# The first way back of an alignment kernel: a part of each step moves from VectorE to TensorE and PSUM

## The reference, cut to what matters

```python
def _pairwise_euclidean(a, b): ...          # D[i, j], 64 x 1601 for each batch
def _dtw_cost(D): ...                       # R[i, j] = D[i, j] + min(R[i-1, j], R[i, j-1], R[i-1, j-1])
def _backtrack(R, T1, T2):                  # from (T1-1, T2-1) back to (0, 0)
    ...
    choice = jnp.argmin(jnp.stack([cd, cu, cl]))      # diagonal, up, left
    ni = jnp.where(choice <= 1, i - 1, i)
    nj = jnp.where((choice == 0) | (choice == 2), j - 1, j)
def _align_one(small, large):
    ...
    expanded = jnp.zeros((T_large, d)).at[j_idx].add(small[i_idx] * valid)
x = x + vmap(_align_one)(ctx_1024, layernorm(x))
x = x + rwkv7(layernorm(x), ...)
x = x + moe_ffn(layernorm(x), ...)
```

## Time and profile before

| what | value |
|---|---|
| median of 3 runs | 1171.64 us |
| span of the profiled execution | 1175.4 us (3.8 above the median, 0.9 above the slowest of the runs) |
| PE busy | 1005.5 us, 86% |
| DVE busy | 660.5 us, 56% |
| ACT busy | 494.2 us, 42% |
| chain that ended last, by engine | PE 55%, DVE 29%, DMA 6%, issue 4%, ACT 3% |
| share of that chain on L841 / L846 | 3% / 2.8% (both ways back) |
| way back of group 0 on DVE | 293.3 to 376.6 us |

### The profile page before, as it was taken

One profiled execution on the slowest core, in us unless ns is written; L12 is line 12 of the kernel. 1 busy time (PEld: TensorE's weight loads), 2 busy tenths in 40 slices (PEclk: granted clock), 3 DMA queues, 4 the chain that ended last, 5 costly groups with the idle time before them and its releaser, 6 DMA issues.

```text
span 1175.4 us, 15523 instructions
## 1 busy us (share of the span) xinstructions
PE 1005.5 (86%) x4892; PEld 598.2 (51%) x4892; DVE 660.5 (56%) x2311; ACT 494.2 (42%) x847; POOL 115.5 (10%) x150
## 2 busy tenths in 40 slices
PE   5886639888891799997899699887999999999998
PEld 2332213333330455553576465645676767676776
DVE  4994949999999776487669612427311111111116
ACT  4885627766781345423242155243222222222221
POOL 1000000000000000000000000000252425242210
PEclk9998979999996799988899799799999999999999
DMA  9999954565876989440050097394121212123115
GB/s 354 324 309 272 274 155 141 154 190 157 237 225 163 327 252 329 135 150 11 1 186 1 0 336 249 104 349 174 49 83 57 83 56 84 56 84 105 32 52 182
DMA packets 123806, 190.47 MB, mean 162 GB/s; under 512 B 9008, under 2 KB 93136, under 8 KB 123728
## 3 DMA queue, kind: packets, MB, share of 16 engines
q1 hardware_dynamic: 117840, 171.13, 47.0%
q0 software_dynamic: 5888, 18.36, 5.1%
HBM read 165.43 MB, written 24.03 MB: 161 GB/s over the span
## 4 chain that ended last, share of the span: by engine, by line
PE 55%; DVE 29%; DMA 6%; issue 4%; ACT 3%; SPq 2%; POOL 0%; DVEq 0%; ACTq 0%; POOLq 0%
PE bank L1816 13%; PE bank L1663 8%; PE bank L1847 7%; PE bank L1684 4%; DVE table L825 4%; PE bank L1808 3%; DMA spaced<-dist 3%; DVE beyond L841 3%; DVE passed L846 3%; PE bank L1827 3%; DVE col_min L818 2%; DVE z L756 2%; PE bank L1590 2%; PE bank L1839 2%; PE bank L1811 2%
## 5 line engine op out<-in xcount | busy, mean ns | idle before, releaser
L1028 DVE TENSOR_TENSOR hid<-bank,act_s 128x352 f32<-128x352 f32 x104 | 54.2, 524 | 220.9 <-PE bank L1816 182.1
L1816 PE MATMUL bank<-w_up,srcT 128*128 x512 | 162.9, 460 | 0.8 <-ACT srcT L1434 0.8
L1574 PE MATMUL bank<-sq,ones 128*64 128x402 f32 (+1 forms) x512 | 101.3, 517 | 38.2 <-ACT sq L1291 38.2
L1442 ACT ACTIVATE act_s<-bank 128x352 f32<-128x352 f32 x104 | 47.9, 463 | 198.4 <-PE bank L1816 127.7
L1816 PEld LDWEIGHTS bank<-w_up,srcT 128*128 128x128 f32 x512 | 96.0, 189 | 47.9 <-issue 4.1
L1590 PE MATMUL bank<-table,ident 128*128 128x402 f32 x144 | 68.5, 560 | 56.3 <-DVE stays L789 51.0
L1568 PE MATMUL bank<-ctxT,latT 128*64 128x402 f32 (+1 forms) x512 | 101.2, 517 | 4.8 <-DMA ctxT<-ctx_tr_dram 4.0
L1663 PE MATMUL bank<-rows_c,on_path 128*64 128x256 f32 (+1 forms) x832 | 100.8, 395 | 2.4 <-DMA rows_c<-ctx_nat_dram 1.6
L1291 ACT ACTIVATE sq<-ctxT 128x1608 f32<-128x1608 f32 x64 | 97.5, 1526 | 8.5 <-DMA ctxT<-ctx_tr_dram 8.5
L1847 PE MATMUL bank<-w_dn,hidT 128*128 (+1 forms) x384 | 93.6, 380 | 0.4 <-DVE y_sb L1042 0.4
L1328 ACT ACTIVATE code<-bank,unpassed 128x402 bf16<-128x402 f32 x72 | 42.1, 589 | 122.9 <-PE bank L1592 122.9
(11 more groups left out here) (292 smaller groups left out, 1619.5 us busy)
## 6 DMA issues: line engine op xcount, KB each, us to landing
rows_c<-ctx_nat_dram SPq DMA_DIRECT2D x32, 896.0 KB
ctxT<-ctx_tr_dram SPq DMA_DIRECT2D x32, 804.0 KB, 8.7
ctxT<-ctx_tr_dram SPq DMA_DIRECT2D x32, 797.0 KB, 7.5
rows_c<-ctx_nat_dram SPq DMA_DIRECT2D x32, 640.0 KB
spaced<-dist SPq DMA_DIRECT2D x128, 101.0 KB, 3.8
w_up<-w_t_dram SPq DMA_DIRECT2D x16, 704.0 KB, 13.3
table<-spaced SPq DMA_DIRECT2D x48, 202.0 KB, 4.2
w_dn<-w_t_dram SPq DMA_DIRECT2D x16, 256.0 KB, 5.8
```

The costliest lines, as they stand in the source:

```text
L1028: e.tensor_tensor(hid[i][:, :], psum[2 * i + 1][:, 0:HH], act_s[i][:, :], ALU.mult).then_inc(hid_done, 1)
L1574: last = e.matmul(ps[b * T:(b + 1) * T, 0:nq], ones[:, 0:T], sq[i][:, b, k, 0:nq], start=False, stop=(k == KC - 1))
L1816: last = e.matmul(psum[2 * i + m][:, 0:HH], srcT[t % 2][:, k, :], w_up[:, bass.ds(ex, 1), m, k, columns], start=(k == 0), stop=(k == KC - 1))
```

## The change

For group 0 only, L841 and its f32 sum go. TensorE now forms code plus twice the position in PSUM (`lay_pair`): an identity in bf16 (`alike`) times the code of two steps, then a product over two partitions (`spot_of`, `spot`) that adds the position, counted from the middle. One call lays the two steps of a pair in one of three banks (psum 5 to 7), and pair k waits until VectorE has finished pair k - 3. VectorE's comparison is one `tensor_scalar` in fp16 on positions counted from the middle (`row_mid`): -60000 where the position is at or above the threshold, 0 elsewhere; the reduction takes `hidden` from SBUF and the sum from PSUM. `threshold0` is fp16. Group 1's way back is as before. Three operations join VectorE's set-up and five join GpSimd's.

```diff
@@ VectorE, align(g) @@
-                e.memset(th[:, STEPS:SLOTS], 2.0 * N + 1).then_inc(back_done, 1)
+                e.memset(th[:, STEPS:SLOTS], 2.0 * N + 1 - (0 if g else MIDDLE)).then_inc(back_done, 1)
                 done()
+                if g == 0:
+                    for k in range(BACK_PAIRS):
+                        for at, step in enumerate(pair_steps(k)):
+                            old, new = th[:, step + 1:step + 2], th[:, step:step + 1]
+                            e.wait_ge(back_done, done.n)
+                            e.stream_shuffle(hidden[:, L:LW], old, RIGHT).then_inc(back_done, 1)
+                            e.tensor_scalar(hidden[:, 0:L], row_mid[:, :], old, -60000.0, ALU.is_ge,
+                                            ALU.mult).then_inc(back_done, 1)
+                            if at == 0:
+                                e.wait_ge(laid, k + 1)
+                            e.wait_ge(back_done, done(2))
+                            i = step % 2
+                            e.tensor_tensor_reduce(passed[:, :], hidden[:, :], back_bank(k)[:, i * LW:(i + 1) * LW], 1.0,
+                                                   -60000.0, ALU.add, ALU.max, new).then_inc(back_done, 1)
...
@@ VectorE, set-up @@
+            e.tensor_copy(alike[:, :], ident[:, :]).then_inc(set_up, 1)
+            e.tensor_scalar(inject0[:, :], inject[:, :], -float(MIDDLE), None, ALU.add).then_inc(set_up, 1)
+            e.tensor_scalar(row_mid[:, :], row2[:, 0:L], -float(MIDDLE), None, ALU.add).then_inc(set_up, 1)
@@ TensorE, align(g) @@
-                for step in range(STEPS):
-                    yield
+                for j in range(STEPS):
+                    if g == 0:
+                        ahead = range(BACK_BANKS) if j == 0 else [BACK_BANKS + j // 2] if j % 2 else []
+                        for k in ahead:
+                            if k < BACK_PAIRS:
+                                lay_pair(k)
+                    yield
+
+            def lay_pair(k):
+
+                steps = pair_steps(k)
+                r0, n, bank = steps[-1], len(steps), back_bank(k)[:, 0:len(steps) * LW]
+                if k == 0:
+                    e.wait_ge(spotted, 5)
+                    e.wait_ge(barred, HALVES)
+                e.wait_ge(coded, r0 // CB + 1)
+                if k >= BACK_BANKS:
+                    e.wait_ge(back_done, back_value(pair_steps(k - BACK_BANKS)[-1]))
+                e.matmul(bank, alike[:, :], code[0][:, r0:r0 + n, 0:LW], start=True, stop=False)
+                e.matmul(bank, spot_of[0:2, :], spot[0:2, 0:n, :], start=False, stop=True).then_inc(laid, 1)
```

More of the change, by code:

```diff
@@ L71 @@
 PASSED = 4096.0
+MIDDLE = SEGS * L
+BACK_BANKS = 3
 HALVES = 2 * CODES
@@ L209, in half_count, with pair_steps, back_value @@
     return g * HALVES + 2 * q + h + 1
+def pair_steps(k):
+    return [STEPS - 1] if k == 0 else [STEPS - 2 * k, STEPS - 1 - 2 * k]
+BACK_PAIRS = (STEPS + 1) // 2
+def back_value(step):
+    return 1 + 3 * (STEPS - step) + max(0, STEPS - max(T, step + 1))
 def dist_slot_value(u):
@@ L329, in build @@
         threshold_at = cursor[0]
-        threshold = [place(f"threshold{g}", [SLOTS]) for g in range(GROUPS)]
+        threshold = [place("threshold0", [SLOTS], F16), place("threshold1", [SLOTS])]
         after = cursor[0]
@@ L383, in build @@
             code.append(place(f"code{g}", [SLOTS, W], BF16))
+        at(table_at[0] + TABLE)
+        alike, spot, spot_of = place("alike", [P], BF16), place("spot", [2, LW], BF16), place("spot_of", [P], BF16)
+        inject0, hidden, row_mid = place("inject0", [STEPS]), place("hidden", [LW], F16), place("row_mid", [L], F16)
+        assert cursor[0] <= table_at[1]
         at(table_at[1])
@@ L503, in build @@
         numbered, shaped, terms_kept, terms_in = sem("numbered"), sem("shaped"), sem("terms_kept"), sem("terms_in")
+        spotted, laid = sem("spotted"), sem("laid")
         x_in = sem("x_in")
@@ L529, in build @@
         BUILT = 17
-        SET_UP = 11
+        SET_UP = 14
         TABLE_IN = [16 * -(-STEPS // FEW_ROWS) * sum(len(sets) for sets in LOADED_WITH[:g + 1]) for g in range(GROUPS)]
@@ L540, in path_bank, with back_bank @@
             return psum[2 + part]
+        def back_bank(k):
+            return psum[5 + k % BACK_BANKS]
         def code_rows(g, q, h):
@@ L579, in gpsimd_program @@
                 e.memset(stays[i][:, :, L:LW], 0.0).then_inc(built, 1)
+            e.memset(spot[0:2, :, :], 2.0 * L).then_inc(spotted, 1)
+            iota(spot_of[0:2, :], [[0, GB], [1, SEGS]], -(SEGS // 2), 0).then_inc(spotted, 1)
+            e.wait_ge(spotted, 2)
+            iota(spot[0:1, :, 0:L], [[0, 2], [2, L]], 2, 0).then_inc(spotted, 1)
+            e.memset(spot[0:2, :, L:LW], 0.0).then_inc(spotted, 1)
+            e.memset(spot_of[0:1, :], 1.0).then_inc(spotted, 1)
             def clear_table(g):
@@ L685, in vector_program @@
             e.tensor_scalar(tie[:, :], ident[:, :], -TIE, None, ALU.mult).then_inc(set_up, 1)
+            e.wait_ge(set_up, SET_UP - 3)
+            e.tensor_copy(alike[:, :], ident[:, :]).then_inc(set_up, 1)
+            e.tensor_scalar(inject0[:, :], inject[:, :], -float(MIDDLE), None, ALU.add).then_inc(set_up, 1)
+            e.tensor_scalar(row_mid[:, :], row2[:, 0:L], -float(MIDDLE), None, ALU.add).then_inc(set_up, 1)
             e.wait_ge(set_up, SET_UP)
@@ L834, in align @@
                 done(g * BACK_INCS)
-                e.memset(th[:, STEPS:SLOTS], 2.0 * N + 1).then_inc(back_done, 1)
+                e.memset(th[:, STEPS:SLOTS], 2.0 * N + 1 - (0 if g else MIDDLE)).then_inc(back_done, 1)
                 done()
+                if g == 0:
[12 more added lines that the diff above has]
+                                                   -60000.0, ALU.add, ALU.max, new).then_inc(back_done, 1)
+                            assert done() == back_value(step)
+                            if step >= T:
+                                e.wait_ge(back_done, done.n)
+                                e.tensor_tensor(new, new, inject0[:, step:step + 1], ALU.max).then_inc(back_done, 1)
+                                done()
+                            yield
+                    assert done.n == BACK_INCS
+                    e.wait_ge(back_done, done.n)
+                    path_features(0)
+                    return
                 for step in range(STEPS - 1, -1, -1):
@@ L903, in path_features @@
                                         passed[:, 0:T])
-                e.stream_shuffle(lim, threshold[g][:, 0:T + 1], FIRST_LANE).then_inc(termed, 1)
+                ends, middle = (lim, 0.0) if g else (hidden[:, 0:T + 1], float(MIDDLE))
+                e.stream_shuffle(ends, threshold[g][:, 0:T + 1], FIRST_LANE).then_inc(termed, 1)
                 e.wait_ge(termed, n())
-                e.tensor_scalar(lim, lim, 1.0, -1.0 - MID, ALU.max, ALU.add).then_inc(termed, 1)
+                e.tensor_scalar(lim, ends, 1.0 - middle, middle - 1.0 - MID, ALU.max, ALU.add).then_inc(termed, 1)
                 e.wait_ge(termed, n())
```

## The result

The changed kernel takes 1184.19 us (median of 8 runs, 1180.69 to 1187.86) beside 1175.2 us for the kernel before in the same comparison (8 runs, 1171.23 to 1181.32): a ratio of 1.0079, 95% interval 1.0060 to 1.0098, some 9 us slower. The profiled executions span 1186.6 and 1175.4 us. The forecast was slower by 4.0, 1175.6 us, with a range of 1169.0 to 1181.0; the sign was right, the size was less than half of what came, and the time lies above the range.

What follows compares the result with a forecast made beforehand. VectorE bounds the stretch at 4.75 us a unit, TensorE afterwards at 5.19. The last refinement comes 5.8 us later, the tail gains 1.8: +4.0 on 1171.64 gives 1175.6 us, range 1169.0 to 1181.0.

Steps and rivals of the forecast that it cites:

- First shuffle of the way back: Set-up: added operations delay the first layer norm by up to 1.0 us, hidden by full DMAs.
- The start: Start of group 0's way back: first reduction 2.05 us late behind pair 0, unit 52's products 3.7 us late.
- The unit: TensorE's unit in the stretch: two pairs of 0.40 us raise it from 4.39 to 5.19 us.
- The end of the stretch: Unit 63's products at 358.2, then pairs, leftovers and a wait for VectorE's step; last refinement at 367.1 us.
- The tail: VectorE's 15 last steps at 0.82 instead of 0.94 us gain 1.8 us; features take 3.43 as before.
- the change of bound from VectorE to TensorE: In the stretch of units, the bound passes from VectorE at 4.75 us a unit to TensorE at 5.19.
- the wait for context that goes: TensorE's wait for unit 56's context vanishes but gives nothing, as TensorE is late by more.
- the bank that costs the reduction nothing: VectorE's reduction reading PSUM instead of SBUF costs about nothing, bounds -0.05 to +0.10 us.
- rival C: VectorE's reduction from a bank is 0.12 us slower, so a step gains nothing: +5.8, 1177.4 us; chance 0.10.
- the table that is not waited for: Group 1's table moves by 5.8 to 382.8 us and stays 1.2 us ahead of VectorE.
- rival B: TensorE bounds but loses less: pair 0.27 us, or pairs keep the code halves' clock up; +1.1, 1172.7 us; chance 0.28.
- Rival A: Pairs cost TensorE almost nothing, running in gaps: -4.8 us, 1166.8 us; faster below 0.22 us a pair; chance 0.17.

Runs made afterwards that it cites:

- e6: Changed kernel with the position product over all 128 partitions, the other weights zero: ratio 1.0081, median 1184.67 us.
- e7: e6 with VectorE's three added set-up operations moved behind its first layer norm: ratio 1.0035, median 1180.16 us.
- e8: e7 with GpSimd's added set-up operations moved later as well: ratio 1.0041, median 1179.01 us.
- e10: e8 with the pairs from the fourth on laid two steps later in TensorE's order: ratio 1.0021, median 1177.24 us.
- e1_setup: Kernel before with only the added set-up operations on VectorE and GpSimd: ratio 1.0017, median 1178.15 us.
- e4: Changed kernel without each pair's position product, so positions are left out of the sum: ratio 1.0024, median 1177.31 us.
- e9: Changed kernel with the pairs from the fourth on laid two steps later in TensorE's order: ratio 1.0056, median 1181.32 us.
- e2: Kernel before with the set-up and TensorE's pairs, which nothing reads and which wait for nothing of VectorE's way back: ratio 1.0067, median 1183.01 us.
- e3: Changed kernel without TensorE's pairs, the reduction reading the code from SBUF, positions left out: ratio 0.9974, median 1173.86 us.
- e5: No pairs on TensorE; GpSimd adds the positions to the code in SBUF, VectorE does the last piece: ratio 1.0251, median 1205.14 us.

## Why the prediction was right in sign and short in size

At group 1's way forward the forecast was +4.0 and the trace has +11.5. The 7.5 us between them, term by term:

- *First shuffle of the way back, forecast no shift: +2.5 us.* I had let full DMAs hide the set-up, "at worst 1.0 shows". The layer norm was 1.33 late. Only some 0.5 of that were VectorE's three operations (e6 against e7); the rest was a thing I had called harmless, GpSimd's operations (e7 against e8). How much of it reached the way back I can't tell, since e8 and e10 start like the kernel before and are 1.8 and 3.0 us late at 160 us: the 2.5 us are in part, perhaps wholly, scatter between executions. What gives such a delay back, in e1_setup, is the wait for unit 56's context; the pairs remove that wait, so in the changed kernel it stays.
- *The start, forecast 5.15 us from first reduction to unit 52's products: 6.73, +1.7 with 0.1 at the first reduction.* That pair 0 stands behind ScalarE's squares was priced right (the first reduction 2.15 late beyond the shift, forecast 2.05), and so was the wait for the third step. What I left out is the clock: behind that wait, of 0.99 us, TensorE worked for 3.7 us at the lower level, and the leftover and the pairs around it took 1.6 us more than at the upper one. In e7 and e8, where the clock holds behind a longer wait, the distance is 5.23; that this is nearly the forecast's 5.15 is in part luck, since their pairs are cheaper.
- *The unit, forecast 5.19 us: 5.38, eleven times 0.19 = +2.1.* The term that was mis-sized is the pair, 0.40 against 0.49 (two a unit: (5.38 - 4.39) / 2). I had taken 0.17 us a product from a row whose neighbours are of one shape; the position product has two rows, its neighbours 128 (e4, e6). The bounds, 0.15 to 0.60, held it.
- *The end of the stretch, forecast 8.9 us from unit 63's products to the last refinement: 9.8, +0.9.* TensorE waited 1.67 us for VectorE's step in front of the pair ahead of the last leftover, a wait that the forecast had, and the clock fell once more (L1688 took 1.33), which it had not. Where the clock holds (e6, e7, e8) it is 8.7, and without the wait (e9) 7.8.
- *The tail, forecast 13.4 us from the last refinement to the features: 13.7, +0.3.* The tensor_scalar was cheaper than forecast, 0.27 for 0.30, but every second step pays 0.11 for its second semaphore: 0.84 a step, not 0.82. The features took 3.42.

Right were the change of bound from VectorE to TensorE, the wait for context that goes, the bank that costs the reduction nothing (so rival C falls, and with it the 65 ns more that the prediction worked out from the Trainium skill, "VectorE: DVE Perf Modes", the section on the TRN2 errata: the reduction takes 0.36 to 0.37 us from either), the table that is not waited for, and the code halves at the lower clock (so rival B's second half falls). Rival A fell with e2: a pair costs twice its break-even of 0.22 us; rival B's pair of 0.27 fell with it. The range failed because it held the spread of a pair's cost but nothing for the hand-overs, which the forecast had seen and priced without the clock. From 400 us on the shift did not simply carry over: +11.5 at 391, +7.1 at group 1's first reduction (567.18, before 560.13), +11.3 at 848 us. Behind 400 us both kernels run the same work. Of the 3.3 us between 745 and 848 us, 2.5 lie in one row of 32 products of the same line, which takes 13.75 us before (769.82 to 783.57, granted clock 1.00) and 16.29 after (777.71 to 794.00, granted clock 0.85). The rest, and why the clock differs there, I leave open.

## What to carry to other kernels

Where one engine has 0.36 us a unit to spare, work moved to it is priced by what its neighbours in the queue cost in the new order, the change of shape and the hand-over with its clock included, not by the product alone. Find the slack first: without the added load (e3) a step 0.15 us shorter, 71 times, was worth 0 to 6 us of the whole, since TensorE's own unit and its wait for context became the next limits. When a buffer's reuse makes a full engine wait for a thinner one, ask for it as late as the consumer allows: some 5 us of this stage came from two steps in the order.

## What the runs showed that was not expected

- Products of 404 bf16 columns hold the next one back by 0.17 us between weights of one shape, and by 0.26 to 0.27 where the weights go from 128 rows to 2 and back, or from 128 columns to 64.
- A wait of 0.99 us on TensorE was followed by 3.7 us at clock 0.54, one of 1.75 us (e4) by the lower level too; behind waits of 1.58 us at the same place (e6, e7, e8), and without one (e9), the clock stayed at 1.00.
- While GpSimd worked in SBUF, some of VectorE's tensor_scalar and tensor_tensor operations there were held, the longest until just behind GpSimd's end: 0.33 us became 1.84, 0.57 became 1.89, 0.36 became 0.76. VectorE's scans and three tensor_scalars of one column did not slow.
- A second semaphore, another engine's, in front of a VectorE operation cost 0.11 us, although it was long given, whether the operation then read a bank or SBUF (e5).
